# A message-passing kernel on one core: two search routines, a check and the order of two engines' work are moved

## The reference

```python
def L0(gat_out, ...):                       # x = x + L0(relu(layernorm(x)))
    h = tanh(gat_out @ W_in + b_in)
    deg = clip(segment_sum(ones, dst), 1.0, None)[:, None]
    decay = relu(clearance)
    for _ in range(12):                     # dt = 0.5
        agg = segment_sum(h[src], dst) / deg
        diff = tanh(gelu(agg @ W1 + b1) @ W2 + b2)
        h = h + (diff - decay * h) * dt
    return h

def gcn_conv(x, W, b):                      # loops are added to src and dst
    norm = rsqrt(deg)[src] * rsqrt(deg)[dst]
    return segment_sum((x @ W)[src] * norm[:, None], dst) + b

def L1(x, ...):                             # x = x + L1(relu(layernorm(x)))
    return gcn_conv(relu(gcn_conv(x, G1, gb1)), G2, gb2)
```

## Time and profile before

| | us |
|---|---|
| median of 3 runs (1275.50 to 1277.84) | 1276.69 |
| the profiled execution, its own time | 1277.91 |
| its span, from first to last instruction | 1276.3 |
| PE busy | 1228.6 |
| DVE busy | 413.0 |
| ACT busy | 302.4 |
| POOL busy | 565.7 |

### The profile page before, as it was taken

The page is one execution under the profiler, slowest core; times in us unless marked ns, Lnnn a source line. Parts: engine busy times, 40 slices in busy tenths (PEclk is TensorE's granted clock), DMA queues, the critical chain, the costliest instruction groups (busy, mean ns, idle before and its releaser), DMA issues.

```text
span 1276.3 us, 17218 instructions
## 1 busy us (share of the span) xinstructions
PE 1228.6 (96%) x6757; PEld 693.6 (54%) x6757; DVE 413.0 (32%) x860; ACT 302.4 (24%) x446; POOL 565.7 (44%) x426
## 2 busy tenths in 40 slices
PE   3799899999999999999999999999999999999998
PEld 1676456564564555645645556455564564555545
DVE  7999314022141131211401313113022142382312
ACT  1798313121131121211311213112121131120100
POOL 6600102845818628368185482771845818600000
PEclk8899999999999999999999999999999999999999
DMA  4000201222222312222222222222322223420101
GB/s 102 2 1 1 65 17 45 36 55 40 35 58 36 55 40 35 58 36 35 59 36 50 44 35 54 40 35 59 36 53 40 35 59 64 94 61 1 51 17 34
DMA packets 106136, 54.58 MB, mean 43 GB/s; under 512 B 13238, under 2 KB 104473, under 8 KB 105964
## 3 DMA queue, kind: packets, MB, share of 16 engines
q0 software_dynamic: 46352, 23.46, 14.2%
q1 hardware_dynamic: 57958, 29.48, 8.6%
q10 hardware_dynamic: 1782, 1.06, 0.3%
HBM read 32.53 MB, written 21.04 MB: 42 GB/s over the span
## 4 chain that ended last, share of the span: by engine, by line
PE 87%; DVE 10%; issue 2%; ACT 1%; DMA 0%; DVEq 0%; SPq 0%; POOL 0%; ACTq 0%; POOLq 0%
PE ps L887 61%; PE ps L951 10%; PE ps L941 9%; DVE scratch L1413 5%; PE ps L800 4%; PE ps L1048 1%; PE ps L930 1%; DVE lo L1396 1%; PE ps L725 0%; DVE state L1681 0%; PE ps L783 0%; DVE cols L1654 0%; DVE adj L1275 0%; DVE ps L1578 0%; ACT scratch L1183 0%
## 5 line engine op out<-in xcount | busy, mean ns | idle before, releaser
L887 PE MATMUL ps<-adj,hi 128*128 128x512 f16 (+2 forms) x2000 | 710.8, 367 | 1.2 <-DVE lo L1396 1.2
L887 PE MATMUL ps<-adj,lo 128*128 128x512 f16 (+2 forms) x1920 | 693.8, 367 | 0.0
L672 POOL DMA_INDIRECT scratch<-state_scratch,tail_rows x264 | 390.7, 1480 | 369.7 <-DMA state_scratch<-state 292.5
L887 PEld LDWEIGHTS ps<-adj,hi 128*128 128x128 f16 x2000 | 194.3, 97 | 220.4 <-issue 13.4
L887 PEld LDWEIGHTS ps<-adj,lo 128*128 128x128 f16 x1920 | 186.8, 97 | 212.9 <-issue 14.6
L1578 DVE TENSOR_TENSOR ps<-ps,bias 128x512 f32<-128x512 f32 (+2 forms) x84 | 53.8, 641 | 499.8 <-PE ps L951 499.8
L1183 ACT ACTIVATE scratch<-ps 128x512 f32<-128x512 f32 (+2 forms) x84 | 46.3, 551 | 582.3 <-DVE ps L1578 581.9
L1174 ACT ACTIVATE scratch<-ps,b1c,cols 128x512 f32<-128x512 f32 (+2 forms) x156 | 107.3, 740 | 176.9 <-PE ps L941 176.1
L951 PEld LDWEIGHTS ps<-w,scratch 128*128 128x128 f32 (+1 forms) x1152 | 138.3, 190 | 14.3 <-issue 5.3
L951 PE MATMUL ps<-w,scratch 128*128 128x128 f32 (+1 forms) x1152 | 143.7, 276 | 0.1
L672 POOL DMA_INDIRECT entry<-state_scratch,tail_rows x88 | 129.7, 1474 | 26.8 <-issue 26.8
(11 more groups left out here) (209 smaller groups left out, 404.6 us busy)
## 6 DMA issues: line engine op xcount, KB each, us to landing
state_scratch<-state SPq DMA_DIRECT2D x55, 256.0 KB, 2.3
scratch<-state_scratch,tail_rows POOLq DMA_INDIRECT x264
state_scratch<-state SPq DMA_DIRECT2D x11, 192.0 KB, 2.0
scratch<-rdeg_scratch SPq DMA_DIRECT2D x1, 1562.5 KB, 8.9
entry<-state_scratch,tail_rows POOLq DMA_INDIRECT x88
state<-in_x_dram SPq DMA_DIRECT2D x5, 256.0 KB
scratch<-in_x_dram SPq DMA_DIRECT2D x5, 256.0 KB
x_scratch<-state SPq DMA_DIRECT2D x5, 256.0 KB, 2.7
```

Of the source, the lines that this page charges most:

```text
L672: nc.gpsimd.indirect_dma_start(tail_sum[i], None, state_dram, bass.IndirectOffsetOnAxis(ap=tail_rows[:, at:at + 1], axis=0), compute_op=AL ...
L887: return nc.tensor.matmul(bank, values[:, k, :], adj[:, k, c0:c0 + n], start=is_first, stop=is_last)
```

## The change

It touches four places. The two tail searches move from ahead of the seven rounds of statistics into them: one to the end of the third round, one to the beginning of the seventh. The sum of the marks on TensorE moves from ahead of group 5 of step 0 to ahead of group 4, and `tail_flag` on VectorE from behind `means(0, 4)` to behind `means(0, 2)`. In the last step the normed rows of groups 3 and 4 are made by ScalarE in place of VectorE, the loops of groups 5 and 6 are added last, `add_input(3)` comes ahead of `means(11, 5)`, and the biases and updates of groups 5 and 6 stand side by side. Between the layers `next_layer_lo` of groups 0 to 4 comes ahead of the two `rows_out`.

```diff
+ACT_NORMS = (3, 4)
+DVE_NORMS = [g for g in range(NG) if g not in ACT_NORMS]
...
@@ tensor, first_step
-                    if g == 5:
+                    if g == 4:
                         pe.wait_ge(s_valid, 1)
...
@@ scalar, step
+                def norm_rows(g):
+                    k0, nt = GROUPS[g]
+                    act.wait_ge(s_fac, 2)
+                    act.wait_ge(s_st[g], STEPS * 16 * parts(g))
+                    for k in range(k0, k0 + nt):
+                        last_ = nc.scalar.activation(state[:, k, :], state[:, k, :], ACT.Identity, bias=ln_b[:, k:k + 1],
+                                                     scale=ln_a[:, k:k + 1])
+                    last_.then_inc(s_ta, 1)
...
                     gelu(t, TAIL)
-                    norm_hi(3)
                     tanh(t, TAIL - 1)
-                    norm_hi(4)
                     tanh(t, TAIL)
+                    for g in ACT_NORMS:
+                        norm_rows(g)
+                        norm_hi(g)
                     norm_hi(5)
...
@@ vector, rounds of statistics
             for g in range(NG):
                 dve.wait_ge(s_x[g], 16 * parts(g))
+                if g == WCOLS + 1:
+                    tail_search(1)
                 last = row_statistics(g)
                 if g >= 2:
                     key_fields(g - 2)
                 if 1 <= g <= WCOLS:
                     key_group(g - 1)
+                if g == 2:
+                    tail_search(0)
...
@@ vector, last_step
                         update(t, g - 2)
+                    if g == TAIL - 1:
+                        add_input(g - 2)
                     means(t, g)
-                    add_loops(g)
-                    if g >= 2:
+                    if g < TAIL - 1:
+                        add_loops(g)
+                    if 2 <= g < TAIL - 1:
                         add_input(g - 2)
...
                 means(t, TAIL)
+                add_bias(t, TAIL - 2)
                 norm_lo(0)
-                add_bias(t, TAIL - 2)
                 norm_lo(1)
                 update(t, TAIL - 2)
+                add_input(TAIL - 2)
                 norm_lo(2)
-                add_input(TAIL - 2)
                 row_factors(12, 20)
-                norm_rows(3)
                 add_bias(t, TAIL - 1)
-                norm_rows(4)
+                add_bias(t, TAIL)
                 update(t, TAIL - 1)
+                update(t, TAIL)
+                add_input(TAIL - 1)
+                add_input(TAIL)
                 norm_lo(3)
-                add_input(TAIL - 1)
                 norm_lo(4)
-                add_bias(t, TAIL)
-                update(t, TAIL)
-                add_input(TAIL)
                 row_factors(20, TILES)
                 norm_rows(5)
                 norm_rows(6)
-                add_loops(TAIL)
                 norm_lo(5)
                 norm_lo(6)
+                add_loops(TAIL - 1)
+                add_loops(TAIL)
...
@@ vector, first_step
                     means(0, g + 2, True)
-                tail_flag()
+                    if g == 0:
+                        tail_flag()
...
@@ vector, between the layers
-                    next_layer_lo(0)
+                    for g in range(TAIL - 1):
+                        next_layer_lo(g)
                     rows_out(TAIL - 1)
-                    next_layer_lo(1)
-                    next_layer_lo(2)
                     rows_out(TAIL)
-                    for g in range(3, NG):
-                        next_layer_lo(g)
+                    next_layer_lo(TAIL - 1)
+                    next_layer_lo(TAIL)
```

More of the change, by code:

```diff
@@ L400, in gnn_kernel @@
         s_t = sem("norm_rows_ready")
+        s_ta = sem("scalar_norm_rows_ready")
         s_z = sem("second_layer_rows_ready")
@@ L1189, in step @@
             def step(t, last):
+                def norm_rows(g):
[6 more added lines that the diff above has]
+                    last_.then_inc(s_ta, 1)
                 def norm_hi(g):
-                    act.wait_ge(s_t, g + 1)
+                    if g in ACT_NORMS:
+                        act.wait_ge(s_ta, ACT_NORMS.index(g) + 1)
+                    else:
+                        act.wait_ge(s_t, DVE_NORMS.index(g) + 1)
                     nc.scalar.activation(tiles_of(hi, g), tiles_of(state, g), ACT.Relu).then_inc(c_hi[0], 1)
@@ L1310, in _ @@
                                 ).then_inc(s_start, 1)
-            for j in range(SETS):
-                dve.wait_ge(s_chunk, WCOLS + j + 1)
-                link(V.tensor_scalar(tail_junk[0:SET_NODES, :], ps[0:SET_NODES, WCOLS + j, 0:CHUNK], tail_first[:, j:j + 1], 0.0,
-                                     ALU.is_lt, ALU.add, accum_out=tail_found[:, j:j + 1]))
-                link(V.tensor_scalar(tail_start[:, j:j + 1], tail_found[:, j:j + 1],
-                                     ps[0:SET_NODES, WCOLS + j, CHUNK + 1:CHUNK + 2], 0.0, ALU.add, ALU.max))
-                V.tensor_scalar(tail_start_i[:, j:j + 1], tail_start[:, j:j + 1], float(EDGES), None, ALU.min
-                                ).then_inc(s_start, 1)
             mv = mean_var[:, :].rearrange("p (k s) -> p k s", s=2)
@@ L1343, in key_fields, with tail_search @@
                 V.tensor_scalar(lane_i[:, q], edge_i[:, q], 7, None, ALU.arith_shift_right).then_inc(s_bits, 1)
+            def tail_search(j):
+                dve.wait_ge(s_chunk, WCOLS + j + 1)
+                link(V.tensor_scalar(tail_junk[0:SET_NODES, :], ps[0:SET_NODES, WCOLS + j, 0:CHUNK], tail_first[:, j:j + 1], 0.0,
+                                     ALU.is_lt, ALU.add, accum_out=tail_found[:, j:j + 1]))
+                link(V.tensor_scalar(tail_start[:, j:j + 1], tail_found[:, j:j + 1],
+                                     ps[0:SET_NODES, WCOLS + j, CHUNK + 1:CHUNK + 2], 0.0, ALU.add, ALU.max))
+                V.tensor_scalar(tail_start_i[:, j:j + 1], tail_start[:, j:j + 1], float(EDGES), None, ALU.min
+                                ).then_inc(s_start, 1)
             for g in range(NG):
                 dve.wait_ge(s_x[g], 16 * parts(g))
+                if g == WCOLS + 1:
+                    tail_search(1)
                 last = row_statistics(g)
@@ L1685, in norm_lo @@
             def norm_lo(g):
-                dve.wait_ge(s_t, g + 1)
+                if g in DVE_NORMS:
+                    dve.wait_ge(s_t, DVE_NORMS.index(g) + 1)
                 dve.wait_ge(c_hi[0], g + 1)
```

## The result

| | before | after |
|---|---|---|
| median of 20 executions | 1276.82 us (1274.69 to 1278.23) | 1274.99 us (1272.44 to 1276.28) |
| ratio of times, 95% interval | 1 | 0.9986 [0.998, 0.9993] |
| profiled execution | 1277.91 us, span 1276.3 | 1274.60 us, span 1272.9 |

The change saves 1.83 us by the medians, half of the 3.7 us forecast. The interval leaves no doubt that it is faster (0.9 to 2.6 us), but the gain is within the 0.2% called no change. The median lies outside the forecast's own range (1272.0 to 1274.0), and inside the wide one (1271.3 to 1275.2) by 0.2 us.

What follows compares the result with a forecast made beforehand. The prediction took TensorE as the bound from about 136 us and VectorE's chain before 133 us. Its terms, 0.5 + 1.72 + 0.9 + 0.57 = 3.7 us, took the median from 1276.69 to 1273.0 us, 8-in-10 range 1271.3 to 1275.2.

Steps and rivals of the forecast that it cites:

- The tail searches: Start, VectorE's rounds of statistics: moving both searches into the rounds brings the first BN_AGGR 0.5 us earlier.
- the rival of a start that loses: Start: first runs or x land 1 to 2 us late, rounds end at 30 to 31, 0.5 becomes 0 to -1; chance 0.10.
- the 0.48: Seventh round: VectorE's 0.48 us wait for ScalarE's copy of the edges, to be filled by the second search.
- the 0.28: Sixth round: VectorE's 0.28 us wait for ScalarE's copy of the edges, to stay since no search is there.
- the gather of the second tail run: Beside the variances: it starts some 3 us later and costs nothing, being first used four batches on.
- The check: Tail group of step 0: moving the marks' sum and flag removes TensorE's wait, 1.72 us saved.
- the last step: Last step: new order and ScalarE's normed rows remove TensorE's wait for `lo` of group 5, 0.9 us saved.
- the layers: Between the layers: earlier `lo` parts remove TensorE's wait at the second group, 0.57 us saved.
- ScalarE did not become the wait: Last step, rival: normed rows take 1 to 2.5 us longer, TensorE waits for group 3, 0.9 lost; chance 0.08.
- GpSimd's gathers of step 1: After step 0's check: they start from the stores of the new state, so they move along with TensorE.
- The rival with a lost stretch: Stage up to 133 us: one more low-clock stretch on TensorE costs 1.7 us, giving 1274.7; chance 0.12 for a loss.

Runs made afterwards that it cites:

- searches ahead again: Changed kernel with its two tail searches put back ahead of the rounds of statistics; median 1274.67 us, ratio to before 0.998.
- searches alone: Kernel before with nothing but the two tail searches moved into the rounds; 1277.74 us, ratio 1.001.
- later weights: Changed kernel with eight loads of weights and biases issued later, by SyncE instead of ScalarE; 1272.17 us, ratio 0.9965.
- later x: Changed kernel with the loads of x for groups 2 to 6 held back until the fourth window search; 1272.58 us, ratio 0.997.
- TensorE kept busy: Changed kernel with the weights loaded later, plus 22 unused 128x128 matmuls in TensorE's idle time; 1272.6 us, ratio 0.9969.
- second gap filled: Changed kernel with weights loaded later, five BN_AGGR moved into the sixth round, first search ahead of its round's fields; 1271.64 us, ratio 0.9963.
- both together: Changed kernel with weights loaded later, the fuller rounds and the extra TensorE matmuls; 1271.44 us, ratio 0.9961.

## Why half of the gain was missing

**The tail searches: this step failed.** The prediction gave them -0.5 us, from "before nothing waited for them, and I take 0.5". The step from "nothing waited" to "it is there early enough" is wrong. No wait at 22.8 only shows that the run had landed by 22.8; the changed kernel asks at 20.9. The term measured +0.91 us (rounds end at 30.93; +0.95 when moved alone), which is the rival of a start that loses, in its size (30 to 31) and its sign (a DMA as releaser ahead of the first keys). It came with 0.10 in the prediction and deserved most of the weight: the row of before from 12 to 20 us, shown above, has the DMA engines at 1.06, and a gather issued there could have been doubted. The rest of the step held: start of the statistics 19.26, the 0.48 filled, the 0.28 left. The gain in the rounds was even larger than 0.5: from the first keys to the end of the rounds it took 7.19 us before and 8.33 after, with 2.02 us of searches inside, so 0.88 were gained (0.39 to 0.98 in the five executions where the first search follows the second keys), against 1.79 lost at the first keys, which began at 22.60 instead of 20.81 (22.83 less the 2.02 of the searches). The prediction also moved the gather of the second tail run by 3 us only; it moved by 6.1 (24.57 to 30.66) and cost nothing, since GpSimd's normed rows still waited 3.14 us for VectorE.

**The check, the last step and the layers: right**, each also alone: 1.78, 0.97 and 0.55 us against 1.72, 0.9 and 0.57. ScalarE did not become the wait. GpSimd's gathers of step 1 moved along, as argued: the first began at 213.58 instead of 215.40.

**The sum.** With the one term replaced, 3.31 - 0.91 = 2.4 us are expected of the change. The same two numbers, how much earlier or later the factors of the norms begin than in before, and 3.31 for the three parts where they are in, stand against all timed kernels:

| kernel | by the two numbers, us | measured by medians | interval of the ratio in us |
|---|---|---|---|
| after | +0.91 - 3.31 = -2.40 | -1.83 | -2.6 to -0.9 |
| searches ahead again | +0.03 - 3.31 = -3.28 | -2.13 | -3.7 to -1.4 |
| searches alone | +0.95 | +0.94 | +0.1 to +2.4 |
| later weights | -0.49 - 3.31 = -3.80 | -4.63 | -6.1 to -2.7 |
| later x | +0.07 - 3.31 = -3.24 | -4.22 | -5.1 to -2.4 |
| TensorE kept busy | -1.19 - 3.31 = -4.50 | -4.21 | -5.5 to -2.4 |
| second gap filled | -1.18 - 3.31 = -4.49 | -5.17 | -6.4 to -3.1 |
| both together | -1.14 - 3.31 = -4.45 | -5.37 | -6.8 to -3.3 |

All eight lie in their intervals. The medians miss by up to 1.2 us, though, to both sides, and it is not shown what makes that up. Part of the agreement of the forecast was luck: the profiled execution took 1274.60 where 1274.2 had been forecast, since 1.0 us that fell out well between the factors and the mark stood against the lost 0.91 and the missing 0.5; and the median is inside the wide range by 0.2 us with the mechanism of the first term wrong in sign.

**The clock.** The rival with a lost stretch was not what happened: in the profiled execution TensorE lost 0.68 us in the batches and gained 1.68 ahead of the mark. From the factors to the last 92x2 pair the twelve other executions took 101.1 to 102.9 us, in no order that was found to go with an edit: the same code of this stage took 101.1 in one part alone and 102.3 in before. From the factors to the mark the thirteen executions took 106.5 to 109.5 us. So this stretch scatters by about 3 us, and what is behind it hardly at all. For the 24 matmuls ahead of the mark the rows show that it is the clock (0.57 and 1.00); for the batches that is argued. That it also explains the leftover of the medians is not shown, and the mean clock of an execution is a poor guide to it: six executions of the kernel kept busy, all at 0.992 or 0.993, scatter from 1271.0 to 1273.2.

## What to carry to other kernels

That nothing waits for a transfer shows that it has landed by the time it is asked for, and no more. Before work is taken from ahead of its first use, bound the landing by that use and look at the share of the DMA engines between issue and use: where they are full, as here (1.04 to 1.06), the work may have been the transfer's cover. And where a transfer is late, look for loads that are issued beside it and needed much later; here eight of them, moved back, ended the rounds 1.39 us earlier (30.93 to 29.54), where moving the searches alone was to bring 0.5.

## What the runs showed of the hardware that was not expected

- A gather issued at 15.43 us took 7.15 us by the chain while the DMA share was 1.04, and at most 5.4 (15.31 to 20.72) with the weights' loads out of the way, at 0.85. (These are means from 12 to 20 us.) Its landing moved between 22.4 and 23.3 us in six executions in which its own code was the same.
- With 22 matmuls added TensorE's granted clock was 1.00 from 33 to 36 us, with TensorE busy for 1.64 of the 3 us, and 0.58 from 36 to 40 us, with TensorE busy for 3.66 of the 4. The mean clock rose from about 0.989 to 0.993 and the time did not fall. The same 24 matmuls took 5.38, 7.06 or 8.35 us in executions whose instructions up to there differ little or not at all.
- Four identity passes of 128x128 on ScalarE beside tanh took 1.64 us without a table load, 0.41 each from start to start.
